# Layer 0 attention: the products with the values at two steps of sixteen, two key blocks at each, where they were at four steps with one

## The reference

```
q, k, v = heads of xn @ Wq + bq, xn @ Wk + bk, xn @ Wv + bv      # 16 heads x 8
scores  = (q k^T + q pos_k^T[bucket] + k pos_q^T[bucket]) * scale  # 512 x 512 per head
p       = softmax(scores)
context = p @ v                                                    # per head, 512 x 8
x       = x + LN(context @ Wo + bo + xn) * ln_scale + ln_bias + (product of xn with sign(weight))
```

## Time and profile before

| | |
|---|---|
| median of 3 runs | 2078.79 us (2075.82 to 2080.17) |
| span of the profiled execution | 2079.5 us |
| layer 0's steady part | 100 to 800 us of it |
| TensorE busy over the span | 1901.5 us, 91% |
| VectorE, ScalarE, GpSimd busy | 80%, 72%, 59% |
| mean granted clock | 0.969 |

### The profile page before, as it was taken

The page is one execution under the profiler, slowest core; times in us unless marked ns, Lnnn a source line. Parts: engine busy times, 40 slices in busy tenths (PEclk is TensorE's granted clock), DMA queues, the critical chain, the costliest instruction groups (busy, mean ns, idle before and its releaser), DMA issues.

```text
span 2079.5 us, 38853 instructions
## 1 busy us (share of the span) xinstructions
PE 1901.5 (91%) x13494; PEld 1465.0 (70%) x13494; DVE 1670.8 (80%) x3871; ACT 1492.8 (72%) x2979; POOL 1217.4 (59%) x1026
## 2 busy tenths in 40 slices
PE   4899999999999999588997999999999888889998
PEld 3677676767777766454695888888887666668797
DVE  7798989999999999367088888888988787764686
ACT  5788888887888888244376677777777677776675
POOL 3878888887878875158064555555555544437300
PEclk7999999999999999699999999999999999999999
DMA  6999898988989885200000000000001000012000
GB/s 189 323 309 323 296 320 291 321 294 308 314 309 321 300 306 193 92 1 22 19 2 6 1 1 1 1 1 1 1 1 32 1 1 1 1 41 82 11 1 41
DMA packets 72264, 263.99 MB, mean 127 GB/s; under 512 B 10822, under 2 KB 30406, under 8 KB 71558
## 3 DMA queue, kind: packets, MB, share of 16 engines
q1 hardware_dynamic: 71126, 256.53, 36.3%
q10 hardware_dynamic: 944, 4.98, 0.6%
HBM read 140.17 MB, written 121.31 MB: 126 GB/s over the span
## 4 chain that ended last, share of the span: by engine, by line
PE 41%; DVE 7%; ACT 6%; POOL 2%; issue 2%; DVEq 0%; POOLq 0%; ACTq 0%
PE PS L157 10%; PE PS L335 8%; PE PS L161 8%; PE PS L163 7%; PE PS L162 7%; ACT AR L167 3%; ACT L167 2%; DVE AR L185 1%; DVE PT L181 1%; DVE DR L181 1%; ACT PT L171 1%; DVE AR L193 1%; POOL AR L176 1%; DVE AR L176 1%; DVE AR L181 0%
## 5 line engine op out<-in xcount | busy, mean ns | idle before, releaser
L167 ACT ACTIVATE AR<-PS,AR 128x512 f32<-128x512 f32 x1024 | 698.5, 690 | 204.0 <-DVE AR L193 91.4
L193 DVE TENSOR_REDUCE AR<-PS 128x1 f32<-128x512 f32 x896 | 615.4, 687 | 91.6 <-PE PS L163 76.0
L335 PE MATMUL PS<-ident,AR 128*128 128x128 f32 x3816 | 582.2, 277 | 32.5 <-DVE PT L181 18.5
L335 PEld LDWEIGHTS PS<-ident,AR 128*128 128x128 f32 x3816 | 444.8, 142 | 127.9 <-issue 45.6
L157 PE MATMUL PS<-AR 128*128 128x128 bf16 (+7 forms) x4126 | 484.8, 357 | 40.0 <-DVE AR L1379 14.6
L181 POOL TENSOR_TENSOR AR<-AR 128x512 f32<-128x512 f32 (+6 forms) x325 | 389.8, 1218 | 199.0 <-DVE AR L181 84.2
L176 POOL TENSOR_SCALAR AR<-AR 128x512 f32<-128x512 f32 (+1 forms) x146 | 256.0, 1754 | 265.6 <-DVE AR L1783 196.4
L171 ACT ACTIVATE AR<-PS 128x512 f32<-128x512 f32 (+3 forms) x596 | 348.5, 587 | 50.9 <-PE PS L157 27.2
L157 PEld LDWEIGHTS PS<-AR 128*128 128x128 bf16 (+4 forms) x4126 | 291.6, 131 | 114.7 <-issue 61.6
L171 ACT ACTIVATE PT<-PS 128x512 fp32r<-128x512 f32 x320 | 191.4, 598 | 161.2 <-PE PS L335 128.7
L181 DVE TENSOR_TENSOR AR<-PS,AR 128x512 f32<-128x512 f32 (+3 forms) x321 | 211.6, 660 | 70.0 <-PE PS L157 61.7
(11 more groups left out here) (175 smaller groups left out, 2982.4 us busy)
## 6 DMA issues: line engine op xcount, KB each, us to landing
scr<-AR SPq DMA_DIRECT2D x128, 800.0 KB, 4.4
XN<-scr SPq DMA_DIRECT2D x85, 768.0 KB, 6.6
AR<-scr SPq DMA_DIRECT2D x43, 768.0 KB, 6.7
AR<-qsc SPq DMA_DIRECT2D x96, 192.0 KB
qsc<-AR SPq DMA_DIRECT2D x16, 384.0 KB, 4.1
qsc<-AR SPq DMA_DIRECT2D x16, 256.0 KB, 4.6
AR<-in_wgu SPq DMA_DIRECT2D x16, 256.0 KB, 3.2
qsc<-AR SPq DMA_DIRECT2D x16, 128.0 KB, 4.5
```

Source lines behind the costliest of these rows:

```text
L167: return ac.e.activation(out, in_, func, bias=bias, scale=scale, accum_out=accum)
L193: return dv.e.tensor_reduce(out, in_, AX.X, ALU.max, negate=True)
L335: return pe.e.transpose(out, in_, ident[0:k, 0:k])
```

## The change

The visits at steps 16G + 21 and 16G + 25 go; the one at 16G + 23 does key blocks 0 and 1, the one at 16G + 27 key blocks 2 and 3. `pv` itself, its waits and its increment are as before.

```diff
@@ l0_pe, the loop over the steps
                 for use in small(u):
                     small_mm(use)
                 G, r = divmod(u - 21, 16)
-                if 0 <= G < 4 * NB and r in (0, 2, 4, 6):
+                if 0 <= G < 4 * NB and r in (2, 6):
+                    pv(G, r // 2 - 1)
                     pv(G, r // 2)
```

## The result

The changed kernel takes 2097.6 us (median of 4 runs, 2094.44 to 2099.41), the kernel before 2079.48 (4 runs, 2075.82 to 2082.17). The ratio is 1.0085, with a 95% interval of 1.007 to 1.010: slower by 18 us. The forecast was 2099.

What follows compares the result with a forecast made beforehand. No engine alone was taken to bound the kernel, but a chain of waits between TensorE, VectorE and ScalarE. 31 groups' delays sum to 20.5 us, added to the 2078.79 median: 2099 us; 8-in-10 range 2078 to 2111.

Steps and rivals of the forecast that it cites:

- The price of the second visit: On TensorE, a visit right behind another costs two passes, 0.86 us; scores to next scores 2.91 us after a wait.
- The Trainium skill's rule: Rival for double visits: weight loads don't overlap, 0.09 us a pass, two passes, 62 places; 2110 us, chance 0.03.
- the chain: Exponential 4 through step 7's scores and double visit to maximum 8: 0.74 + 2.91 + 1.97 = 5.62 us; maxima 8 to 12 6.34.
- What the edit frees at step 5: The 1.07 us freed on TensorE becomes waiting for exponential 4; step 7 can't come further forward.
- by kind: Four kinds of sixteen-step group in a sequence's 64 steps; maximum 8 later by 0.57, 0.79, 0.38 and 0.51 us.
- The sum: Over 31 groups in layer 0's attention: 4.7 + 7.1 + 3.8 + 4.9 = 20.5 us later.
- nothing is given back: After step 12 scores to maximum is 1.97 us as before, so no loss is recovered and none added.
- VectorE's idle time: VectorE's waits for TensorE (L157 and L580) in 100 to 800 us rise from 41 us to about 65.
- Signs that I had named: Profile after: x16 visits of about 1.9 us, double steps of 2.8 to 2.95, a wait before step 7's scores, 1.2 us lumps.
- TensorE's busy share: In the attention stretch, it falls to about 96% of a longer stretch.
- busy shares: Rival: TensorE, 97% busy, sets the time by its total work; 13 us saved, 2066 us, chance 0.13.
- VectorE never waits for GpSimd: Reading of the waits in 100 to 800 us, held against the rival that the lag is absorbed (2079 or 2089, chance 0.14).

Runs made afterwards that it cites:

- the fourth buffer: The changed kernel with four buffers for the exponentials instead of three: 2094.70 us, ratio 1.0080 to the kernel before.
- the doubles at 6 and 10: The changed kernel's two double visits moved from steps 7 and 11 to even steps 6 and 10: 2082.80 us, ratio 1.0031 to the kernel before.
- the two halves: Two runs against the kernel before, each joining one pair of visits: only the first, at step 7, 2090.77 us; only the second, at step 11, 2078.81 us.

## Why the prediction was right

*The price of the second visit.* 0.86 us from the end of the layer: the x16 rows last 1.90 where the x8 rows last 1.05, and scores 7 to scores 8 are 2.91 us, the number of the prediction. The Trainium skill's rule ("TensorE: Matmul & The Clock Gate", Part 3, The mechanism) that weights load beside running matmuls only in another row group did not show as a cost here beyond the spacing of rows 8, which already holds the loads: with it the double step would have taken 2.91 + 0.18. The bare odd step that the prediction had only by difference (about 0.9) is 0.88, so a visit alone is 1.98 - 0.88 = 1.10 us and a joined one saves 0.24 and not 0.21; the chain doesn't use that term.

*What the edit frees at step 5 goes into a wait, mostly.* A visit of 1.1 us is gone there, but step 7 starts only 0.29, 0, 0.55 and 0.43 us sooner behind maximum 4, by kind. In the second kind the step that waits is 6 and the exponential is number 3. Steps 5, 6 and 7 of such a group, in the kernel before:
```profile
378.43 0.44 PE L577 MATMUL PS<-ident,XN 128*128 128x128 f32 x2 [0.32 <-ACT AR L167]
...
380.48 0.44 PE L577 MATMUL PS<-ident,XN 128*128 128x128 f32 x2
...
381.67 0.39 PE L577 MATMUL PS<-ident,XN 128*128 128x128 f32 x2
```
and in the kernel after, steps 6 and 7:
```profile
385.27 0.44 PE L577 MATMUL PS<-ident,XN 128*128 128x128 f32 x2 [0.91 <-ACT AR L167]
...
386.46 0.39 PE L577 MATMUL PS<-ident,XN 128*128 128x128 f32 x2
```
From step 6 to 7 it is 1.19 us in both, and the whole second visit comes on top. That is why this kind grew by 0.86 us. The chain there runs through exponential 3, which the prediction had missed: step 7 starts 0.88 us after exponential 4 (385.58) and not 0.74. That its number for this kind, 0.79, is so close is chance.

*The chain.* Maxima 4 to 8 by kind after, less before, against the prediction: 6.87 - 6.24 = 0.63 (0.57), 7.05 - 6.19 = 0.86 (0.79), 6.33 - 5.96 = 0.37 (0.38), 6.32 - 5.83 = 0.49 (0.51). Maxima 8 to 12: 6.33 - 6.24 = 0.09 (0.10). That the bf16 products are a link of it is shown by moving them (0.40 us from scores to maximum, in the kernel with double visits; a gain in the kernel before too), that the transposes aren't by the fourth buffer (no change), that most of the cost is the place by the doubles at 6 and 10 (6.5 us), and that the first pair has nearly all of it by the two halves (14.4 and 2.5 us).

*The sum.* 20.5 us were expected for the layer; from the first to the last of the 512 maxima it is 796.0 - 779.9 = 16.1.
- Maxima 4 to 8 gave 16.2 of the 17.4 expected. The prediction took all groups by their kind and held that the six that differ change the sum by under 1 us. Read one by one from the trace before they lie between -0.2 and +0.9 us and take 2.1 from it: a misreading of 2 us, of which 1.2 showed.
- Maxima 8 to 12 gave 2.0 of 3.1. The first sixteen steps, which have no visits, were 0.7 us shorter in this execution, and the last group isn't in the pattern.
- The other 2.1 us are the one step that failed: "nothing is given back". 12 to 16 gave back 1.7 us, nearly all in steps 44 to 48 of a sequence (see the last section), and the rest 0.3.

The span is 18.1 longer and not 16.1: 0.7 us less before the first maximum and 2.7 more behind the last, where nothing was edited. I take these for the scatter of one execution: over the traces of all runs the time behind the last maximum lies between 1245.8 and 1251.6 us. So the forecast of +20 against +18 is right by its mechanism, 4.4 us too high for the layer, and closer than that by 2 us of luck.

*VectorE's idle time* was forecast at 65 us and is 65.2.

*Signs that I had named.* Visits of x16 at two steps, 2.84 to 2.91 us a double step, a wait before the scores of step 7 (in the second kind of group it is TensorE's own time that is last there), lumps of up to 1.3 us: all are there. Not as said is TensorE's busy share, 662.49 of 700 us or 94.6%, where I had about 96%.

## What to carry to other kernels

In a pipeline of engines with two or three buffers between them, put long pieces of work singly and where their engine waits; joining them saves the switch (0.24 us here) and loses the neighbour's time that the lump overruns (up to 0.86). To price it, walk the chain once around all engines, from the wait in front of the lump to the operation that restarts the wait, and hold it against the distance in the trace: busy shares gave the wrong sign here. Behind a lump, issue first what the slowest engine waits for: exchanging two lines in TensorE's order was worth 10.7 us without any lump and 15 with two, though it left some 13 us of what the lumps cost, while a buffer that removed a wait of 55 us on another engine was worth nothing. To say that a cure has removed a cause, apply it to the kernel without the cause too.

## What the runs showed of the hardware

A VectorE operation on 4 elements per partition can last until a GpSimd operation that is already running ends. In the kernel before, in order of time, VectorE and then GpSimd:
```profile
418.45 0.98 DVE L185 SCALAR_TENSOR_TENSOR AR<-AR 128x4 f32<-128x4 f32 x1
```
```profile
416.03 3.38 POOL L181 TENSOR_TENSOR AR<-AR 128x192 f32<-128x192 f32 x3 [1.36 <-DMA AR<-scr]
```
The small operation ends at 418.45 + 0.98 = 419.43, GpSimd's at 416.03 + 3.38 = 419.41. In the kernel after, GpSimd stood idle at that point and four such operations together took 0.75 us:
```profile
424.39 0.75 DVE L185 SCALAR_TENSOR_TENSOR AR<-AR 128x4 f32<-128x4 f32 x4
```
```profile
426.15 1.05 POOL L181 TENSOR_TENSOR AR<-AR 128x512 f32<-128x512 f32 x1 [2.05 <-DVE AR L181]
```
Such operations of more than 0.3 us number five in the layer before and three after; each ends 17 to 21 ns behind the end of a GpSimd operation. Their excess over 0.16 us is 3.1 us before and 1.4 after, and that difference is the 1.7 us given back.

The other runs bear this out. Over all 13 traces there are 55 such operations, each ends 15 to 24 ns behind the end of a GpSimd operation, and none of the short ones lies inside one. In the ten traces whose visits stop at step 11 or before, the distances from maximum 44 to 48 of the eight sequences add up to between 48.97 and 51.93 us; less the excess of that trace they are 48.6 to 48.8 in all ten. So the held operations cost time one for one there, and how many are held differs from trace to trace (an excess of 0.4 us with the first pair joined, 1.9 with the second): what was given back here is where GpSimd happened to stand, not something that double visits buy.

No row of waits shows it, since the time is booked as VectorE's work: "VectorE never waits for GpSimd" was true of the rows and wrong of the engine.

The Trainium skill ("SBUF — State Buffer", SBUF: two separate sides) has the rule: VectorE and GpSimd share a pair of SBUF ports as an exclusive lock, and whichever starts first of a GpSimd operation that reads SBUF and a VectorE operation with two SBUF inputs (or of a GpSimd operation and a VectorE operation in a two-port mode) makes the other wait for the whole instruction. The trace agrees in what it can show: the held operations read two SBUF tensors; the large adds of every step read one side from PSUM, run beside GpSimd all the time and keep their 0.68 us. I had not applied it, since I looked for waits only. I made no run that takes GpSimd's operation away from that place alone, so the lock as the cause is read from the ends of the held operations and not tested.
